# Three semaphore waits per block left out of TensorE's queue in a two-layer mixture-of-experts kernel

## The reference, cut to what matters

```python
x = x + _L0_conv_ref(_ln_c(x), L0_conv_codebook, L0_conv_bias)
t = t + _L0_ffn_ref(_ln_t(t), L0_ffn_Wg, L0_ffn_W1, L0_ffn_W2)
...
x = x + _L1_conv_ref(_ln_c(x), L1_conv_bias, L1_conv_up_filter, L1_conv_down_filter)
t = t + _L1_ffn_ref(_ln_t(t), L1_ffn_router_w, L1_ffn_w1, L1_ffn_w2, L1_ffn_w3)
```

## Time and profile before

| what | value |
|---|---|
| median of 3 runs | 1527.68 us (1527.48 to 1532.9) |
| span of the profiled execution | 1634.3 us |
| TensorE busy, share of the span | 1137.5 us, 70% |
| VectorE busy | 976.8 us, 60% |
| GpSimd busy | 735.5 us, 45% |
| ScalarE busy | 641.0 us, 39% |

### The profile page before, as it was taken

The page is one execution under the profiler, slowest core; times in us unless marked ns, Lnnn a source line. Parts: engine busy times, 40 slices in busy tenths (PEclk is TensorE's granted clock), DMA queues, the critical chain, the costliest instruction groups (busy, mean ns, idle before and its releaser), DMA issues. The chain is left out here.

```text
span 1634.3 us, 29161 instructions
## 1 busy us (share of the span) xinstructions
PE 1137.5 (70%) x6195; PEld 884.1 (54%) x6196; DVE 976.8 (60%) x3803; ACT 641.0 (39%) x1295; POOL 735.5 (45%) x703
## 2 busy tenths in 40 slices
PE   1697212222229999999848989899794699998930
PEld 0697212221229999998725555455452576777720
DVE  6664324443546666665465777668764677776744
ACT  2454223332314444444343655555554243343310
POOL 0332255556644444444351364574536555554420
PEclk9998555555559999999959999899896799999975
DMA  8242762221112222222150021221102222222249
GB/s 209 70 110 69 186 184 53 50 54 45 41 43 66 62 62 63 63 61 62 49 171 22 15 68 40 50 56 29 29 19 56 65 78 69 72 74 68 71 115 259
DMA packets 138877, 123.73 MB, mean 76 GB/s; under 512 B 65813, under 2 KB 119310, under 8 KB 137408
## 3 DMA queue, kind: packets, MB, share of 16 engines
q1 hardware_dynamic: 107149, 72.91, 18.6%
q0 software_dynamic: 19968, 39.44, 7.7%
q10 hardware_dynamic: 11667, 10.46, 2.3%
HBM read 72.74 MB, written 51.06 MB: 76 GB/s over the span
## 5 line engine op out<-in xcount | busy, mean ns | idle before, releaser
L645 POOL DMA_INDIRECT routed<-r_xn,r_slot x320 | 342.4, 1070 | 343.9 <-DVEq L634 219.9
L1020 POOL DMA_INDIRECT answers<-e_y,e_dest x152 | 146.0, 960 | 199.9 <-ACT e_y L1145 194.2
L1020 POOL DMA_INDIRECT answers<-c_c x152 | 146.1, 961 | 145.1 <-ACT c_c L1145 92.0
L1429 PE MATMUL c_pz<-c_c,down 116*120 116x512 f32 (+1 forms) x392 | 193.4, 610 | 0.0
L1197 DVE COPY e_ht<-e_ps_ht 128x512 f32<-128x512 f32 x152 | 105.2, 692 | 122.8 <-PE e_ps_ht L1066 120.1
L1076 PE MATMUL e_ps_y<-w,e_ht 128*128 x1216 | 160.8, 275 | 0.3 <-DVE e_ht L1197 0.3
L1076 PEld LDWEIGHTS e_ps_y<-w,e_ht 128*128 128x128 f32 x1216 | 147.8, 192 | 0.8 <-issue 0.6
L1403 PE MATMUL c_py<-c_xh,gl 121*116 121x512 f32 (+1 forms) x196 | 120.4, 614 | 35.9 <-DVE c_xl L1532 34.1
L1542 DVE SCALAR_TENSOR_TENSOR c_c<-c_a 116x1024 f32<-116x1024 f32 (+1 forms) x60 | 75.0, 1250 | 69.6 <-ACT c_a L1487 60.0
L608 PE MATMUL r_ps_rank<-r_picked,before 120*120 120x32 bf16 (+1 forms) x40 | 9.7, 243 | 151.7 <-DVEq L587 104.5
L1140 ACT ACTIVATE e_h<-e_ps_h 128x512 f32<-128x512 f32 x154 | 92.0, 597 | 58.3 <-PE e_ps_h L1056 56.1
(11 more groups left out here) (206 smaller groups left out, 2999.9 us busy)
## 6 DMA issues: line engine op xcount, KB each, us to landing
answers<-answers SPq DMA_DIRECT2D x32, 480.0 KB
e_xg<-routed SPq DMA_DIRECT2D x159, 66.0 KB
c_c<-routed SPq DMA_DIRECT2D x159, 66.0 KB
c_w<-in_w SPq DMA_DIRECT2D x26, 393.8 KB
routed<-r_xn,r_slot POOLq DMA_INDIRECT x320
c_x<-in_xh SPq DMA_DIRECT2D x4, 1170.0 KB
w1l<-in_w SPq DMA_DIRECT2D x2, 2048.0 KB, 10.6
out<-x ACTq DMA_DIRECT2D x16, 240.0 KB
```

The source lines that it names most:

```text
L645: ro.nc.gpsimd.indirect_dma_start(ro.xs, bass.IndirectOffsetOnAxis(ap=ro.slot[0:px, q, c:c + 1], axis=0), ro.xn[0:px, q, k, t, :], None).t ...
L1020: ex.nc.gpsimd.indirect_dma_start(ex.ys, bass.IndirectOffsetOnAxis(ap=ex.dest[:, s:s + 1], axis=0), ex.y[:, s, :], None).then_inc(ex.store ...
L1429: ins = nc.tensor.matmul(ps_z[q % 3][0:rows, :], r.down[0:PPX, m * TPX:m * TPX + rows], c[0:PPX, p % R, :], start=p == ROWS * q, stop=p == ...
```

## The change

It takes three of the four second waits out: that of `turn_x` for `x_split`, that of `first_product` for `hid_ready` and that of `turn_h` for `ht_ready`. The wait of `second_product` for `y_ready` stays, and so do all first waits. `turn_x` loses its argument b. No matmul, vector operation or DMA is added, taken away or moved.

```diff
-    def turn_x(b, s, turn_no, early):
+    def turn_x(s, turn_no, early):
+
         if early and room is not None:
             room("x", s)
         pe.wait_ge(ex.x_in[s % U], 16 * (turn_no + 1))
-        if not early:
-            pe.wait_ge(x_split, b - 1)
         nc.tensor.transpose(ex.ps_x[s % 2][:, 0:P], ex.xg[:, s % U, 0:P], r.ident[:]).then_inc(x_turned, 1)
 
     def first_product(b, s, w, early):
         if early and room is not None:
             room("h", s)
         pe.wait_ge(x_split, b + 1)
-        if not early:
-            pe.wait_ge(hid_ready, b - 1)
         i = s % 2
...
         pe.wait_ge(hid_ready, b + 1)
-        if not early:
-            pe.wait_ge(ht_ready, b - 1)
         for c in range(chunks):
...
     for s in range(2):
-        turn_x(s, s, 0, True)
+        turn_x(s, 0, True)
...
-    turn_x(2, 2, 0, False)
+    turn_x(2, 0, False)
...
         turn_h(b, s, first and s < 2)
-        turn_x(b + 3, s + 3, it + (1 if s + 3 >= U else 0), False)
+        turn_x(s + 3, it + (1 if s + 3 >= U else 0), False)
```

## The result

The changed kernel runs in 1519.68 us at the median of five runs (1511.05 to 1519.82), the kernel before beside it in 1528.87, so the medians lie 9.2 us apart. One run of the kernel before took 2114.7 us, far above the others, and counts in that median but not in the ratio. The ratio is 0.9911, with a 95% interval of 0.9888 to 0.9933: 0.89% or 13.6 us faster (0.0089 x 1528.87). The means of the runs, without that one, are 12.3 us apart (1516.9 and 1529.2), and a repetition further down has the ratio 0.9909 and medians 14.0 us apart; so I go by the ratio. The forecast was 1523.7 us, 4.0 us under its reference, in a range of 1503 to 1533. So direction and range held, and the gain is more than three times the forecast. It lies above the 0.5% that a measurement can tell, a case that had been given 0.27, and above 8.4 us, the upper end of the prediction's own account.

What follows compares the result with a forecast made beforehand. Experts 0 was taken as bound by the array; experts 1 had 54 us above its floor, split between VectorE and sequencer issue. Terms 2.3 + 3.5 + 2.6 = 8.4 us, times 0.48, gave 4.0: 1527.7 - 4.0 = 1523.7 us, range 1503 to 1533.

Steps and rivals of the forecast that it cites:

- a case that had been given 0.27: Whole kernel faster by more than 0.5% (7.6 us): 0.05 from the prediction's own account plus 0.22 from the sequencer as bound.
- the prediction's own account: Experts 1: removed waits save sequencer time at starved places, 0 to 8.4 us, value 4.0; chance 0.53.
- nothing in experts 0, all in experts 1, no order changed: Experts 0 gains 0 (bounds 0 to 1 us), experts 1 gains 4.0 us; the removed waits never stop TensorE's queue.
- third rival: Both expert stages: shifted code makes each turn stop once for instruction loading, 25 us slower, 1552.8 us; chance 0.08.
- second rival: Experts 1: in timed runs the sequencer keeps its lead, so the gain is hidden, 1527.7 us; chance 0.17.
- first rival: Experts 1: the sequencer paces it throughout, so all 24.6 us of issue idle time go, 1503.1 us; chance 0.22.
- the halving: Experts 1: 8.4 us times 0.48, issue's share of idle time, gives 4.0 us; the rest lost waiting for VectorE.
- The sum: Experts 1: 2.3 us before second product L1076, 3.5 before first product L1054, 2.6 before transposes L1066; together 8.4 us.
- the price of one entry: TensorE's sequencer: one removed wait saves 0.1 us, its distance to the next entry, rather than its 51 ns duration.
- estimate of 2 us: Experts 1: gain if the profile stretches all sequencer work like the branch, 208 ns against about 108 ns in the skill.
- The rule on the wait queue: TensorE: the sequencer passes a waiting matmul, so removed waits gain 0; the trace disagreed, and it stood as second rival.
- Its signs: Block distance: experts 0 stays 2.15 us, experts 1 falls 1.875 to about 1.85 (1.7: first rival); issue idle before L1076, L1054 falls.

Runs made afterwards that it cites:

- a repetition further down: The changed kernel, unedited, timed again against the kernel before: median 1517.65 us, ratio 0.9909 (0.9895 to 0.9924).
- single-stage kernels: The kernel before with the three waits left out in one stage only: experts 1 alone, ratio 0.9895; experts 0 alone, ratio 0.9990.
- the second profile: The kernel before, unedited, profiled once more: span 1529.5 us; timed at 1531.39 us, ratio 0.9994.
- the kernel with more waits: The kernel before with two further, already covered waits at each of the three places, 24 more entries a turn: 1561.84 us, ratio 1.0191.

## Why the forecast was right, and where it was too small

**Right: nothing in experts 0, all in experts 1, no order changed.** The single-stage kernels show the first two. The third follows from the code, where an earlier wait of the queue asks for as much; no run tests it by itself. The third rival (a stop for code in every turn) did not occur: 73 packets as before, and no block of a turn is longer on average. The second rival (hidden anyway) falls with a ratio whose interval ends at 0.9933. The first (the sequencer paces experts 1 throughout) was wrong as it was put, since five blocks of eight stand at the array's pace in the second profile (four at 1.49 us, one at 1.52). Its price of 24.6 us was idle time of a disturbed execution; the kernel with more waits shows what that state looks like when it is real.

**Right by luck: the range.** The measured 13.6 us, and the lower end of their interval (0.67%, 10.2 us), lie above the 8.4 us with which the prediction's own account ended. The range holds them because it had been drawn down to 1503 us for the first rival, whose mechanism is not what happened.

**Wrong: the halving.** The sum was 8.4 us and was multiplied by 0.48, on the ground that the rest of the idle time was VectorE's and that time saved would be lost there. In the second profile VectorE's part is 4.0 of 21.3 us, not 26.6 of 51.2, and those 4.0 carry a wrong label. In the third block, where the sequencer does stand for the gate product, savings are not lost: behind the release at 1333.7 us it still has the entries of L1044, L1074 and L1052 to handle before the first product at 1334.87. Two of the three removed waits stand between the release and that product, and both paid. Without the halving the forecast would have been 1519.3 us, 0.4 us from the measured median, but 8.4 us of gain against 13.6 by the ratio; and those 8.4 us were put together from the wrong places, as the next point shows. The prediction had noted that the span lay 106.6 us above the median; the right use of that was to distrust the idle times by releaser, not to carry their shares over.

**Wrong: the places in the sum.** The sum counted the 84 gaps that rows 6 list, at 0.1 us each, and they are gaps of the disturbed execution. By step of the turn, 31 of them lie in the first block, 27 in the block of L1033, only 6 in the third block and 20 elsewhere: 3.1, 2.7, 0.6 and 2.0 us. By the means above the three blocks gave 0.27, 0.19 and 0.21 us a turn; over 19 turns that is 5.2, 3.6 and 3.9 us, with 0.9 from the block two steps behind L1033's. So the third block is the term that was missed most.

The first block was too small as well, and there the sum does not follow its own words. They hold that waits which ride on register operations are worth nothing, and that L1066's gap at the turn end gives nothing since branch and table load make it; but 11 of the 26 places in front of L1066 that it counts are at the turn end, and so are 17 of the 23 in front of L1076, where L1044 was a register operation. The sequencer's entries at the turn end in the second profile (columns as in rows 3), where those of L1044 and L1064 were made for the waits:

```profile
L1084 PEldq TENSOR_LOAD <-table x1: 298/298/298, 1329.4 to 1329.4; - x1
...
L985 PEldq COMPARE_BRANCH  x1: 208/208/208, 1329.9 to 1329.9; - x1
...
L1064 PEldq ALU_OP  x1: 36/36/36, 1330.2 to 1330.2; - x1
...
L1044 PEldq ALU_OP  x1: 32/32/32, 1330.5 to 1330.5; - x1
...
L1052 PEldq EVENT_SEMAPHORE  x1: 51/51/51, 1331.3 to 1331.3; - x1
```

The changed kernel has none of the last three there. L1052's is gone, and the thresholds that other waits still need are worked out one block later, where the lead covers them:

```profile
L1059 PEldq ALU_OP  x1: 32/32/32, 1327.4 to 1327.4; - x1
```

So three entries leave the dearest place of the turn, and its first block gains 0.27 us on average, about 0.1 each: the largest part of the 0.72 us a turn. That branch and load make a gap does not mean that an entry behind them is free; they are in line, and each one adds to it. The whole is 0.72 us x 19 turns = 13.7 us, against 13.6 by the ratio.

**Right: the price of one entry.** 0.1 us, its distance to the next, is about what a removed entry gave at the starved places (0.27 for three in the first block, 0.21 for two in the third), not the 51 ns of its own duration; left out alone, one gave 0.05 to 0.13 us there. The prediction's estimate of 2 us (half of its 4.0, not of its sum), for a profile that stretches the sequencer's work, has nothing left for it: the branch took 208 ns in the second profile too, an execution that lasted as long as the others (1531.52 us), and what the distances in the profiles say (13.7 us) is what the timed runs say.

**The rule on the wait queue.** The prediction set a row against the Trainium skill (Perfetto Trace Analysis, Tensor Engine Instruction), by which a matmul that waits is queued and the sequencer goes on, so that the gain would be 0. The measurement sides with the row in the block seen here: in the second profile too the entry of L1064 is handled at 1333.3 us and the next one, L1044's, only at 1333.7, when the gate product has ended (1333.62) and the transposes start.

**Its signs.** It named 1.85 us a block in experts 1 as its own case and 1.7 as the first rival's. Since an undisturbed execution had 1.67 before and 1.58 after, neither sign could be read; a sign given as a difference (0.03 us a block forecast, 0.09 found) could. The idle time by issue fell from 17.3 to 4.0 us, but 13.1 us came back under VectorE's name with the sequencer as the cause, so that sign could not be read by its label either.

## What to carry to other kernels

Before costing idle time by what it was waiting for, compare the profiled execution with the timed runs; here it was 7% longer, its stalls were not those of an ordinary execution, and only order, counts and the shortest distances could be used. For small instructions in a loop, lay the starts of one repeated matmul side by side over a whole turn: the blocks that exceed the array's own distance are the places where the sequencer is late, each entry there costs about its distance to the next one, and elsewhere, in this kernel, nothing. Then look at all the entries of that place, not at those of the change alone: here one table load in a turn too many was worth another 0.6% (0.9909 against 0.9848).

## What had not been expected of the hardware

A wait that is already met was not free on TensorE: 24 further entries a turn made experts 1 12% longer (295.1 against 263.2 us) while every engine did the same work. A load of one table word into a register held TensorE's sequencer for 0.30 us and cost 0.34 us a turn at the turn end, and nothing two steps earlier. And a wait listed against an engine can be another's: 13.1 us listed behind VectorE fell to 1.0 us when TensorE's own sequencer had one load less, with VectorE's work unchanged.
